# A post-norm attention and feed-forward layer on eight cores: an outer product moved one tile later, and fused row statistics split in two

## What is computed

```python
nx = (x - mu) * rsqrt(var + EPS) * gamma + beta
q, k, v = nx @ Wq.T + bq, nx @ Wk.T + bk, nx @ Wv.T + bv    # 16 heads of 64
q, k = softmax(q, axis=-1), softmax(k, axis=-1)             # over the 64 of a head
attention = einsum('bnhd,bnhl->bhdl', k, v)                 # sum over the 2048 rows
y = einsum('bnhd,bhdl->bnhl', q, attention)
x = layernorm(x + x @ Wh.T + bh + y)
h = relu(x @ quantize(W1).T + b1)                           # weights in {-1, 0, 1}
x = layernorm(x + h @ quantize(W2).T + b2)
```

## Time and profile before

| | us |
|---|---|
| median of two runs | 9109.65 |
| the two runs | 8648.14 and 9571.17 |
| the profiled execution | 8689.69 |
| its span on core 1, the slowest | 8687.8 |
| spans of the other cores | 8638.4 to 8684.9 |
| TensorE busy | 7552.3 (87%) |
| VectorE busy | 3066.5 (35%) |
| ScalarE busy | 1968.1 (23%) |

### The profile page before, as it was taken

How to read it: one execution, slowest core, us unless ns; L and a number is a source line. 1 busy time by engine, 2 the same in 40 slices (tenths; PEclk the granted TensorE clock), 3 DMA queues, 4 the chain that set the end, 5 groups by cost and what they waited for, 6 DMA issues and landing times.

```text
span 8687.8 us, 121979 instructions; the slowest of 8 cores (8638.4 to 8687.8 us)
## 1 busy us (share of the span) xinstructions
PE 7552.3 (87%) x46099; PEld 4294.4 (49%) x46099; DVE 3066.5 (35%) x5103; ACT 1968.1 (23%) x3453; POOL 110.1 (1%) x212
## 2 busy tenths in 40 slices
PE   2788888888899999999834999999999999999998
PEld 1333333333344444444423666666666666666665
DVE  6444444444444444444465212221222122211221
ACT  1122222222122222222200222222222222222222
POOL 0000000000000000000000000000000000000000
PEclk9889999999999999999955999999999999999999
DMA  1111111111011111111122000000000000000000
GB/s 59 49 33 32 35 37 35 35 32 35 25 35 35 35 35 35 35 35 35 36 84 75 16 15 20 20 20 11 20 20 20 11 20 20 20 11 20 20 20 11
DMA packets 74482, 259.65 MB, mean 30 GB/s; under 512 B 12303, under 2 KB 12455, under 8 KB 73902
## 3 DMA queue, kind: packets, MB, share of 16 engines
q1 hardware_dynamic: 45742, 151.12, 6.3%
q0 software_dynamic: 28160, 100.72, 3.2%
HBM read 184.67 MB, written 67.12 MB: 29 GB/s over the span
## 4 chain that ended last, share of the span: by engine, by line
PE 79%; DVE 13%; issue 3%; ACT 3%; DVEq 1%; DMA 0%; ACTq 0%; POOL 0%; SPq 0%; POOLq 0%
PE P_K L64 29%; PE P_V L64 28%; PE P_T L64 13%; DVE ar L64 6%; PE P_A L64 5%; PE P_SP L64 5%; DVE a L64 3%; DVE B L64 2%; ACT a L64 1%; DVE sm L64 1%; DVE AW L64 1%; DVEq L60 1%; ACT B L64 1%; DVEq L63 0%; ACT ar L64 0%
## 5 line engine op out<-in xcount | busy, mean ns | idle before, releaser
L64 DVE TENSOR_TENSOR B<-ar,B 128x256 bf16<-128x256 f32 (+1 forms) x1152 | 592.6, 514 | 2836.6 <-ACT B L64 2809.6
L64 PE MATMUL P_K<-AW,a 128*128 128x512 bf16 x6144 | 1488.4, 402 | 59.9 <-DVE a L64 59.9
L64 PE MATMUL P_V<-AW,a 128*128 128x512 bf16 x6144 | 1392.3, 384 | 0.0
L64 PE MATMUL P_T<-id,ar 128*128 128x128 f32 x3328 | 570.0, 317 | 678.6 <-DVE ar L64 458.9
L64 PE MATMUL P_K<-AW,B 128*128 128x512 bf16 x4096 | 1072.1, 385 | 79.6 <-DVE B L64 79.4
L64 PE MATMUL P_V<-AW,B 128*128 128x512 bf16 x4096 | 1070.2, 384 | 0.0
L64 PEld LDWEIGHTS P_K<-AW,a 128*128 128x128 bf16 x6144 | 609.6, 102 | 884.5 <-issue 319.2
L64 PEld LDWEIGHTS P_V<-AW,a 128*128 128x128 bf16 x6144 | 584.9, 99 | 790.5 <-issue 176.7
L64 PE MATMUL P_T<-a,AW 128*128 128x256 bf16 x8192 | 972.7, 273 | 0.0
L64 PEld LDWEIGHTS P_T<-a,AW 128*128 128x128 bf16 x8192 | 801.5, 98 | 188.4
L64 PEld LDWEIGHTS P_T<-id,ar 128*128 128x128 f32 x3328 | 431.7, 162 | 842.5 <-issue 836.1
(11 more groups left out here) (67 smaller groups left out, 3682.3 us busy)
## 6 DMA issues: line engine op xcount, KB each, us to landing
ar<-x SPq DMA_DIRECT2D x128, 512.0 KB, 4.1
ar<-W POOLq DMA_DIRECT2D x64, 512.0 KB, 3.9
x2scr<-ar POOLq DMA_DIRECT2D x64, 512.0 KB, 5.2
ar<-W SPq DMA_DIRECT2D x64, 512.0 KB, 3.7
ar<-x2scr SPq DMA_DIRECT2D x64, 512.0 KB, 4.2
out<-ar POOLq DMA_DIRECT2D x64, 512.0 KB, 5.0
ar<-Wk SPq DMA_DIRECT2D x8, 512.0 KB, 4.0
ar<-Wv SPq DMA_DIRECT2D x8, 512.0 KB, 3.8
```

The source lines that it names most:

```text
L64: ins = getattr(h, meth)(*args, **kw)
```

## The change

It has two parts. First, the 48 matmuls into P_A, with the emptying of P_A at a batch's end, become a function `emit_A(j)`, which `emitB1(j+1)` calls after its own K and V projections and ahead of the transposes; the last tile's is called at the end of `emitB1` as before. Buffers are protected accordingly. Second, each fused statistic becomes separate instructions: in `ln_stats` a multiply and two sums; in stage 2 and in `epi` an addition, a multiply and two sums.

```diff
         def ln_stats(y, src_ap, tmp_ap, dst_sc, dst_bi, waits):
+            ev_sq = sd.op("vector", "tensor_tensor", out=tmp_ap, in0=src_ap,
+                          in1=src_ap, op=ALU.mult,
+                          waits=waits + [need(("ar4", y))], inc="v")
             ev_1 = sd.op("vector", "reduce_sum", out=c_s1(y), in_=src_ap,
                          axis=AX.X, waits=waits + [need(("s1", y))], inc="v")
-            ev_2 = sd.op("vector", "scalar_tensor_tensor", out=tmp_ap,
-                         in0=src_ap, scalar=1.0, in1=src_ap, op0=ALU.mult,
-                         op1=ALU.mult, accum_out=c_s2(y),
-                         waits=waits + [need(("ar4", y))], inc="v")
+            ev_2 = sd.op("vector", "reduce_sum", out=c_s2(y), in_=tmp_ap,
+                         axis=AX.X, waits=[ev_sq], inc="v")
...
+        def emit_A(j):
+            y = j % 2
+            b, tib = j // TPB, j % TPB
+            ek16 = B16[:, 0:2048]
+            v16 = B16[:, 2048:4096]
+            ev_el, ev_vl = evs["split", j]
...
+            protect(("ar", 6 + y), ev_A)
+            protect(("ar", 2 + y), ev_A)
+            protect(("ar4", y), ev_A)
+            protect(("b16", 0), ev_A)
+            protect(("b16", 1), ev_A)
+            if tib == TPB - 1:
...
         def emitB1(j):
...
             ev_v = proj(P_V, nxT_hi, nxT_lo, "Wv",
                         ev_wready["Wv"] + [need("P_V")])
+            if j >= 1:
+                emit_A(j - 1)
             quads = trans_nx1_pe(j + 1) if j + 1 < NT else None
...
             if quads is not None:
                 trans_nx1_evac(j + 1, quads)
-            ev_A = None
-            for h in range(H):
...
+            evs["split", j] = (ev_el, ev_vl)
+            if j == NT - 1:
+                emit_A(j)
...
-            ev_r1 = sd.op("vector", "scalar_tensor_tensor", out=AR[y][:, :],
-                          in0=AR[y][:, :], scalar=1.0, in1=P_V[:, :],
-                          op0=ALU.mult, op1=ALU.add, accum_out=c_s1(y),
-                          waits=[ev_y, need(("s1", y))], inc="v")
+            ev_r1 = sd.op("vector", "tensor_tensor", out=AR[y][:, :],
+                          in0=AR[y][:, :], in1=P_V[:, :], op=ALU.add,
+                          waits=[ev_y], inc="v")
             protect("P_V", ev_r1)
...
+            ev_sq = sd.op("vector", "tensor_tensor", out=AR[4 + y][:, :],
+                          in0=AR[y][:, :], in1=AR[y][:, :], op=ALU.mult,
+                          waits=[ev_r1, evt], inc="v")
+            ev_1 = sd.op("vector", "reduce_sum", out=c_s1(y), in_=AR[y][:, :],
+                         axis=AX.X, waits=[ev_r1, need(("s1", y))], inc="v")
+            ev_2 = sd.op("vector", "reduce_sum", out=c_s2(y), in_=AR[4 + y][:, :],
+                         axis=AX.X, waits=[ev_sq], inc="v")
+            ev_bi = ln_finalize(y, ev_1, ev_2, c_rs2(y), c_bi2(y))
...
+                ev_r2 = sd.op("vector", "tensor_tensor", out=xs[:, :],
+                              in0=xs[:, :], in1=P_O[sub][:, :], op=ALU.add,
+                              waits=[evs["ffn2end", s]], inc="v")
                 protect(("PO", sub), ev_r2)
...
+                ev_sq = sd.op("vector", "tensor_tensor", out=AR[4 + y][:, :],
+                              in0=xs[:, :], in1=xs[:, :], op=ALU.mult,
+                              waits=[ev_r2, need(("ar4", y))], inc="v")
+                ev_1 = sd.op("vector", "reduce_sum", out=c_s1(y), in_=xs[:, :],
+                             axis=AX.X, waits=[ev_r2, need(("s1", y))], inc="v")
+                ev_2 = sd.op("vector", "reduce_sum", out=c_s2(y),
+                             in_=AR[4 + y][:, :], axis=AX.X, waits=[ev_sq],
+                             inc="v")
+                ev_bi = ln_finalize(y, ev_1, ev_2, c_rs2(y), c_bi2(y))
```

More of the change, by code:

```diff
@@ L526, in trans_nx1 @@
             trans_nx1_evac(i, trans_nx1_pe(i))
+        def emit_A(j):
[4 more added lines that the diff above has]
+            ev_el, ev_vl = evs["split", j]
+            ev_A = None
+            for h in range(H):
+                hp = (h % 2) * 64
+                for pi, (lo, ro) in enumerate(((0, 0), (1024, 0), (0, 1024))):
+                    w = [ev_el, ev_vl]
+                    if tib == 0 and h == 0 and pi == 0:
+                        w += [need("P_A")]
+                    ev_A = sd.op("tensor", "matmul",
+                                 out=P_A[hp:hp + 64,
+                                         (h // 2) * 64:(h // 2) * 64 + 64],
+                                 lhsT=ek16[:, lo + h * 64:lo + (h + 1) * 64],
+                                 rhs=v16[:, ro + h * 64:ro + (h + 1) * 64],
+                                 start=(tib == 0 and h <= 1 and pi == 0),
+                                 stop=(tib == TPB - 1 and h == H - 1 and pi == 2),
+                                 tile_position=(0, hp), skip_group_check=True,
+                                 waits=w, inc="pe")
+            protect(("ar", 6 + y), ev_A)
[4 more added lines that the diff above has]
+            if tib == TPB - 1:
+                e = None
+                for h in range(H):
+                    hp = (h % 2) * 64
+                    c = h // 2
+                    src = P_A[hp:hp + 64, c * 64:c * 64 + 64]
+                    dhi = A_sb[hp:hp + 64,
+                               b * 2048 + c * 128 + hp:b * 2048 + c * 128 + hp + 64]
+                    dlo = A_sb[hp:hp + 64,
+                               b * 2048 + 1024 + c * 128 + hp:
+                               b * 2048 + 1024 + c * 128 + hp + 64]
+                    eh = sd.op("vector", "tensor_copy", out=dhi, in_=src,
+                               waits=[ev_A], inc="v")
+                    e = sd.op("vector", "tensor_tensor", out=dlo, in0=src,
+                              in1=dhi, op=ALU.subtract, inc="v")
+                protect("P_A", e)
+                evs["Asb", b] = e
         def emitB1(j):
@@ L933, in epi @@
                 y = sub
[L934 to L938, removed]
-                protect(("PO", sub), ev_r2)
[L940 to L945, removed]
+                ev_r2 = sd.op("vector", "tensor_tensor", out=xs[:, :],
+                              in0=xs[:, :], in1=P_O[sub][:, :], op=ALU.add,
+                              waits=[evs["ffn2end", s]], inc="v")
+                protect(("PO", sub), ev_r2)
+                ev_sq = sd.op("vector", "tensor_tensor", out=AR[4 + y][:, :],
[7 more added lines that the diff above has]
+                ev_bi = ln_finalize(y, ev_1, ev_2, c_rs2(y), c_bi2(y))
                 protect(("s1", y), ev_bi)
@@ L950, in epi @@
                              op0=ALU.mult, op1=ALU.add,
-                             waits=[ev_bi, need(("ar", 6 + sub))], inc="v")
+                             waits=[ev_bi, ev_2, need(("ar", 6 + sub))], inc="v")
                 protect(("ar", 2 * p + sub), ev_o)
```

5 lines of the change are left out of this document (removed).

## The result

| us | before | after |
|---|---|---|
| median of all runs | 8787.45 (10 runs) | 9632.9 (11 runs) |
| lowest and highest | 8646.0, 9595.27 | 9096.18, 9851.49 |
| the profiled execution | 8689.69 | 9105.9 |
| its span, and the shortest span of a core in it | 8687.8, 8638.4 | 9104.0, 9061.1 |

The change makes the kernel slower. The ratio is 1.0524, with a 95% interval from 1.0506 to 1.0543. The time compared is then about 9100 us against 8647, some 450 us more; 8961 was predicted, 292 more. 9100 lies in the upper part of the range.

A forecast was written before the change was run, and what follows sets the result against it. TensorE was taken as the bound. Terms of 44 (copy), 51 (batch ends), 0 (stage 1 statistics), 176 (feed-forward) and 21 (stage 2) sum to 292 us, on a base of 8669: 8961 us, range 8850 to 9170.

The forecast's parts named there:

- the feed-forward term: Feed-forward pair boundaries: split statistics add 5.5 us a pair with nothing covering them, 176 us in all (145 to 179).
- K's start hangs on VectorE's queue: Stage 1: VectorE's five queued instructions release K's projection, so taking P_A out of the end gains nothing there.
- the wait that goes is won: Rival, stage 1: TensorE's order holds K, so 215.3 us come back; +33 us, 8702 in all; chance 0.06.
- The sign that I named for it: Feed-forward pair boundaries: TensorE's wait for B ahead of P_K grows from 2.95 to about 8.5 us.
- The batch ends: Stage 1: emptying P_A ahead of the next softmax costs 16.9 us, three times, 51 us (45 to 57).
- the copy's wait: Stage 1: exp k's copy waits for P_A until T+1.2 (T: V's projection ends); 0.7 us a tile, 44 us.
- the clock of stage 1: K's first matmuls lose 1.57 us after each stop, as before, so no added cost; bounds -97 to +97 us.
- stage 2: Split statistics exceed the slack ahead of q's transposes by 0.33 us a tile, 21 us (0 to 56).
- the rival of a clock that falls there: Rival, stage 2: added idle tips the clock, K loses 1.57 us in 62 tiles; 9058 us; chance 0.13.
- The statistics of stage 1, at nothing: First normalisation: one added reduction, 1.3 to 1.4 us, lies beside K's projection and costs 0.
- The fused form and the plain multiply have the same length: VectorE statistics: fused square 1226 ns and plain multiply 1225 ns, so a split adds only the reduction.
- the rival of the short multiply: Rival, VectorE statistics: plain multiply takes half the fused one's time, 0.61 us less a square; 8901 us; chance 0.03.

The follow-up runs named there:

- x4: Changed kernel with fused statistics kept and a second buffer for exp k and v on odd tiles; span 8733.6 us, ratio to before 1.0126.
- x5: x3 with the 32 emptying instructions of P_A put behind the work K's projection waits for; span 8694.2 us, stage 1 2056 us against 2111.
- x3: Changed kernel with fused statistics kept and one semaphore signal for P_A's 48 matmuls; span 8755.8 us, stage 1 2111 us.
- x8: Before, with P_A's matmuls between K's and V's projections, VectorE low parts earlier, fused feed-forward statistics beside the next pair's hidden blocks; 8362.03 us, ratio 0.967.
- x1: Kernel before with only the statistics split as in the change, P_A's matmuls not moved; span 8882.2 us.
- x7: Changed kernel, statistics still split, with the feed-forward statistics and output moved beside the next pair's hidden blocks; span 8805.1 us, feed-forward 3871 us.

## Why the prediction was right or wrong

**Right: the direction, its causes, the feed-forward term.** What decided was the reading that K's start hangs on VectorE's queue, and not on TensorE's order; the rival "the wait that goes is won" is out, and x4 shows why: without P_A in the gap and without the wait for the buffer the gap is 6.09 us, as before. The split instructions on the path cost 5.47 us a pair (predicted 5.5, 176 us), from the first hidden block to the first matmul that waits for B. The sign that I named for it was wrong: the wait itself is 5.9 us and not 8.5, since the hidden blocks ahead of it take 2.9 us longer, which no term of mine had; why their clock is low in after and not in before, no run shows. The batch ends cost 24.74-7.57=17.2 us each (predicted 16.9), 52 us for 51, and x5 shows that this is the place of the emptying.

**The size was off, 292 against about 450 us, by two mis-sized steps.** Term by term, measured less predicted, core 5: the copy's wait +40 us, the batch ends +1, the clock of stage 1 +46, stage 2 +30, the feed-forward stage +36, the rest +6; 159 in all, and 292+159=451. The base hid a part of it: 8669 is the mean of 8648.1 and of the profiled 8689.7, 22 above 8647.

*"So the copy, 1.05 us long, starts at about T+1.2 and ends at T+2.25"*: it starts at T+1.92. I took the 1.0 us of P_A's matmuls plus a signal; but each of the 48 signals its own end, and the last signal arrives 1.92 us after the first matmul starts. The gap grew by 1.42 us and not 0.7: 59x1.42=84 us for 44. x3 shows it: with one signal the copy starts at T+1.06. It could have been read from before, where the first CAST of A_sb, which waits for P_A's last signal, starts at 1322.05, after 0.34 us idle for it. The row ahead of it on TensorE's timeline, at this same place of before, is

```profile
1320.14 0.96 PE L64 MATMUL P_A<-B 128*64 128x64 bf16 x48 [3.29 <-DVE B L64]
```

so 1.91 us lie between the start of the 48 and the arrival of the last signal. The Trainium skill (TensorE: Matmul & The Clock Gate, "The cost: per-tile semaphore tail") names the mechanism, increments that serialise at 26.3 ns each, and says that one on the last matmul is enough. By its figure 47 fewer would save 1.24 us, an estimate; x3 saves 0.85, or 0.018 us for each, and the measurement decides.

*The clock: "I take the same cost."* It is not the same in any stage. In stage 1 K's first 24 matmuls take 7.47 us on average for 6.73: 62x0.74=46 us. A stop of 3.3 us with P_A's work behind it was replaced by one of 5.5 without. In x3, with a stop of 4.7 us, it is 7.27; in x4, with 4.1, 6.91; in x8, with 2.0, 5.43. In the feed-forward stage the period of a pair grew by 6.6 us, of which 5.5 are the instructions; the other 1.1, 31x1.1=35 us, are matmuls at low clock for longer behind the wait (2.84 us for 16 of P_A, 1.91 before). I had argued that the clock is low there already, which says nothing of how long it stays low.

Stage 1 then adds up: 84+52+46=182 for 183 measured. The feed-forward stage: 31x6.6=205, and the last pair's tail; measured 212.

*Stage 2.* The wait of q's transposes is 0.2 us on core 0, 0.4 on core 5 and 0.5 on core 3 on average over all tiles (predicted 0.33). But I had the rival of a clock that falls there as one of all 62 tiles or none, K losing 1.57 us. It falls in some, and K loses nothing (5.27 as before): on core 3 29 of 64 tiles have the A_sb matmuls at more than 2.0 us, before 9, and their gap is 9.70 us against 8.21 in the others. On core 5 the gap's mean went from 7.90 to 8.68 us: 62x0.78=48 of the 51 us (21 predicted). On cores 0, 2, 4 and 6, with 18 to 21 such tiles, it cost 21 to 25, so there the term was right.

*The statistics of stage 1, at nothing*: right, 4 us in x1. *The fused form and the plain multiply have the same length*: right, 1.22 to 1.23 us each at the boundary above, so the rival of the short multiply is out. The 6 us in the rest were not in the sum.

What x7 adds is that it is not the amount but the place: the same split statistics cost 212 us between the pairs, and beside the hidden blocks the stage is 77 us shorter than before, within 4 us of x8 with the fused ones (3871 and 3867).

## What to carry to other kernels

Before moving work off a wait, ask what else ends at the same moment: here VectorE's in-order queue ended with TensorE's, so taking TensorE's wait away won nothing (x4), and reordering the queue's own entries, with P_A's matmuls between the projections and one signal for all 48, won 3.3% (x8). A consumer that moves later keeps its buffer longer, and the buffer comes free with its last signal, not with its last matmul: count the signals. A stop of TensorE costs more than its length, here for K's first 24 matmuls from 0.2 us behind a stop of 2.0 to 2.2 behind one of 5.5 (5.43 and 7.47 us on average against 5.27), so a term for the clock needs its own range and not "the same as before".

## What was not expected of the hardware

48 matmuls of 64x64 take 0.97 us and their 48 signals 1.92 us from the same start, 0.04 us each; with one signal the waiting engine starts 1.06 us after the start. Stage 2's low clock comes and goes from tile to tile at nearly the same idle time: 9 tiles of 64 before, 18 to 29 after or in x1, with only 0.1 to 0.5 us more idle each; what tips one tile and not the next, no run here shows.
